# Five of eight gate products on GpSimd instead of three

## The reference

```python
# window attention: 8x8 windows, 4 heads of 16 channels, relative bias
x = x + conv(_ln_c(x))           # qkv, softmax(q k^T * scale + bias) v, w_proj, b_proj
# mixture of experts on the 64-channel tokens
t = _to_tokens(x)
router_probs = softmax(_ln_t(t) @ router_w + router_b)
top_p, top_i = top_k(router_probs, 2);  top_p = top_p / sum(top_p)
expert_out = einsum('bnd,edc->bnec', _ln_t(t), expert_w) + expert_b
t = t + einsum('bnk,bnkc->bnc', top_p, gathered expert_out)   # 8 experts, 2 per token
```

## Time and profile before

| | |
|---|---|
| three runs | 1201.91, 1205.79 (median), 1210.96 us |
| profiled execution, own time | 1205.98 us |
| its span | 1204.0 us |
| granted TensorE clock, mean | 0.977 |
| PE busy | 1052.5 us (87%) |
| DVE busy | 890.6 us (74%) |
| ACT busy | 745.5 us (62%) |
| POOL busy | 418.6 us (35%) |

### The profile page before, as it was taken

How to read it: one execution, slowest core, us unless ns; L and a number is a source line. 1 busy time by engine, 2 the same in 40 slices (tenths; PEclk the granted TensorE clock), 3 DMA queues, 4 the chain that set the end, 5 groups by cost and what they waited for, 6 DMA issues and landing times.

```text
span 1204.0 us, 39111 instructions
## 1 busy us (share of the span) xinstructions
PE 1052.5 (87%) x16838; PEld 605.8 (50%) x16838; DVE 890.6 (74%) x1443; ACT 745.5 (62%) x1217; POOL 418.6 (35%) x421
## 2 busy tenths in 40 slices
PE   1588889999999999999998999899998999899754
PEld 1355555555554555555554555555554555555311
DVE  3246687688878877788877867789877877788652
ACT  0257776677766766777766666767766766766400
POOL 0000244333443234333344234333443244333543
PEclk9999999999999999999999999999999999999778
DMA  5000656677878766677777757677878766677887
GB/s 179 2 1 20 150 131 149 157 179 183 194 179 196 170 163 155 170 174 179 188 186 186 174 138 170 158 176 188 196 177 194 163 159 167 165 159 173 182 195 172
DMA packets 49255, 192.48 MB, mean 160 GB/s; under 512 B 10558, under 2 KB 10814, under 8 KB 32572
## 3 DMA queue, kind: packets, MB, share of 16 engines
q1 hardware_dynamic: 49084, 189.98, 66.4%
HBM read 154.04 MB, written 18.87 MB: 144 GB/s over the span
## 4 chain that ended last, share of the span: by engine, by line
PE 83%; issue 8%; DMA 3%; DVE 3%; POOL 2%; ACT 1%; SPq 1%; POOLq 0%; DVEq 0%; ACTq 0%
PE bank L591 18%; PE bank L491 12%; PE bank L506 11%; PE bank L482 6%; PE bank L523 6%; PE bank L469 5%; PE bank L530 5%; PE bank L442 5%; PE bank L541 3%; DMA gz<-gates_dram 2%; PE bank L550 2%; PE bank L568 2%; PE bank L577 2%; PE bank L418 2%; PE bank L433 1%
## 5 line engine op out<-in xcount | busy, mean ns | idle before, releaser
L591 PE MATMUL bank<-gz,wex 64*64 64x512 f32 x2048 | 259.9, 612 | 11.1 <-DVE ob L1053 10.9
L900 POOL TENSOR_TENSOR gz<-gz,tt 128x1024 f32<-128x1024 f32 x96 | 233.6, 2435 | 79.3 <-DMA gz<-gates_dram 79.3
L1029 DVE TENSOR_TENSOR probs<-bank,mx 128x1024 f32<-128x1024 f32 x128 | 156.7, 1225 | 114.1 <-PE bank L506 111.2
L741 ACT ACTIVATE pt<-bank 128x512 f32<-128x512 f32 x256 | 151.8, 593 | 143.3 <-PE bank L506 143.0
L1044 DVE TENSOR_TENSOR gz<-gz,tt 128x1024 f32<-128x1024 f32 x160 | 198.9, 1261 | 13.1 <-DMA gz<-gates_dram 13.1
L872 POOL TENSOR_TENSOR tt<-prj,xs 128x512 f32<-128x512 f32 x64 | 80.6, 1283 | 355.8 <-ACT prj L758 355.8
L1022 DVE TENSOR_REDUCE mx<-bank 128x16 f32<-128x1024 f32 x128 | 156.2, 1220 | 40.6 <-PE bank L491 39.5
L506 PE MATMUL bank<-cst,probs 128*128 128x128 f32 x1024 | 167.3, 286 | 2.9 <-issue 2.0
L491 PE MATMUL bank<-km,qs 32*64 32x128 f32 x4096 | 149.9, 282 | 13.4 <-issue 13.4
L506 PEld LDWEIGHTS bank<-cst,probs 128*128 128x128 f32 x1024 | 113.0, 142 | 84.6 <-issue 74.4
L491 PEld LDWEIGHTS bank<-km,qs 32*64 32x64 f32 x4096 | 116.2, 136 | 62.8 <-issue 62.8
(11 more groups left out here) (111 smaller groups left out, 1423.9 us busy)
## 6 DMA issues: line engine op xcount, KB each, us to landing
gz<-gates_dram SPq DMA_DIRECT2D x256, 512.0 KB, 9.0
xs<-in_x SPq DMA_DIRECT2D x32, 512.0 KB, 8.9
tx<-tt SPq DMA_DIRECT2D x128, 128.0 KB, 2.8
out<-ob SPq DMA_DIRECT2D x128, 128.0 KB, 10.0
gz<-in_rel SPq DMA_DIRECT2D x1, 2048.0 KB, 9.9
gates_dram<-gt_rs SPq DMA_DIRECT2D x32, 64.0 KB
cst<-in_consts SPq DMA_DIRECT2D x1, 359.0 KB, 3.0
tt<-in_weights SPq DMA_DIRECT2D x4, 64.0 KB, 2.6
```

Source lines behind the costliest of these rows:

```text
L591: last = mm(bank[64 * x:64 * x + 64, Y_BANK + a, :], wex[64 * a:64 * a + 64, e, :], gz[64 * a:64 * a + 64, s.pair(e)[1], e % 2, x * CH:(x ...
L741: af(pt[g % 2][:, u % 2, :, :, :, :].rearrange("p j h x q -> p (j h x q)"), bank[:, PT_BANK, :], ACT.Copy).then_inc(pt_ready, 1)
L900: tt_(gz[:, k, e % 2, :], gz[:, k, e % 2, :], tt[s.buf(4)][:, :], op=ALU.mult).then_inc(z_pool, 1)
L1029: tt_(probs[g % 2][:, :, :, :].rearrange("p h w (m k) -> p (h w m) k", k=N), two_banks(S_BANK).rearrange("p (c k) -> p c k", k=N), mx[g % ...
```

## The change

Products 3 and 6 go from VectorE to GpSimd. On GpSimd, 6 is put ahead of 7 and 3 behind 1. On VectorE, product 5 and the last `normalise` of a strip are issued at the end of the step in which they become possible instead of at the start of the next one; product 3's place there is gone.

```diff
-        POOL_Z = [1, 4, 7]
+        POOL_Z = [1, 3, 4, 6, 7]
...
                 if s[6].on:
+                    gated(s[6], 6)
                     gated(s[6], 7)
                 if s[5].on:
                     gated(s[5], 1)
+                    gated(s[5], 3)
...
                 s = st.strips()
-                if s[4].on:
-                    normalise(s[4], 3)
-                if s[6].on:
-                    gated(s[6], 5)
                 if s[3].on:
                     row_max(s[3], 3)
...
-                if s[6].on:
-                    gated(s[6], 6)
                 if s[4].on:
                     move_logits(s[4])
...
                     gated(s[5], 2)
-                    gated(s[5], 3)
+                if s[3].on:
+                    normalise(s[3], 3)
+                if s[5].on:
+                    gated(s[5], 5)
```

## The result

Over several runs the changed kernel took 1255.55 us in the median (1249.11 to 1261.01), the kernel before 1203.85 us (1195.08 to 1210.96); the ratio is 1.0431, with an interval of 1.0338 to 1.0525. It is 52 us slower. The profiled execution took 1261.01 us against 1205.98, with a span of 1259.2 us: 55.2 us more. The forecast was 1263.

A forecast was written before the change was run, and what follows sets the result against it. TensorE was taken to bound the kernel, with 83% of the chain that ended last. 29 steps x 2.6 = 75 us, plus 2, less 20 coming back, gave 57 us on 1205.98: 1263 us, range 1235 to 1292.

The forecast's parts named there:

- Step 1: VectorE: two products leave, off TensorE's path, where VectorE waits for TensorE anyway; worth 0.
- Step 2: Product 6 on GpSimd ahead of 7: product 1 starts later, vr released later, keys late; +0.3 us a step (0 to 0.5).
- Step 3: Product 3 on GpSimd holds an instruction of VectorE's top-2 chain, delaying shift and group 1's scores; 2.3 us a step.
- Step 4: VectorE's product 5 and normalise 3 at the end of the step; 0.
- Step 5: GpSimd's sum: two products more, 4.7 us a step, against 10.35 us idle ahead of place_gates; 0.
- What comes back: TensorE's mid-group waits, taken as late instructions, hidden by the new wait: 20 of 22.7 us back (0 to 23).
- The sum: Whole kernel: 2.6 us in 29 steps, 75 us, plus 2, less 20 given back: 57 us slower, 1263 us.
- rival C: Collision as forecast, and TensorE's clock falls: 25 us more if every second step pays, 1288; every step 1312; 12%.
- Rival A: VectorE keeps the port while instructions are queued, GpSimd's products wait, waits ahead of L482 vanish: 1176, faster; 4%.
- Rival B: Product 3 misses the top-2 chain and runs beside row_max and shift, which are not held: 1206 to 1215; 7%.

The follow-up runs named there:

- experiment 4: Kernel before, three products on GpSimd, with GpSimd's product 1 moved behind place_gates: 1169.99 us, ratio 0.9773.
- experiment 6: Changed kernel with GpSimd's products 1 and 3 both moved behind place_gates: 1174.47 us, ratio 0.9778 to the kernel before.
- experiment 3: Kernel before with VectorE's new order alone, all five products staying on VectorE: 1201.20 us, ratio 1.0026.
- experiment 2: Kernel before with product 3 alone moved to GpSimd, behind product 1: 1238.85 us, ratio 1.0361.
- experiment 5: Changed kernel with GpSimd's product 3 moved behind place_gates: 1211.67 us, ratio 1.0086 to the kernel before.
- experiment 7: Changed kernel with product 3 replaced by two equally long GpSimd memsets that read nothing from SBUF: 1216.37 us, ratio 1.0126 to the kernel before.

## Why the prediction was right

**Step 1 (VectorE's two products are worth 0)** held. The wait for TensorE ahead of shift 3 grew from 3.09 to 3.62 us, and experiments 4 and 6 give the same time with three and with five products on GpSimd.

**Step 2 (product 6, +0.3 us a step).** Size about right, the way there another: L1000 does not slip in between 6 and 7 but loses the seam and is held for a whole product. So mq does not pass at the next seam, with vr held in its place, as the step had it; mq is asked for later and is itself held for 1.92 us. In the step shown, TensorE's wait for the keys is 1.21 us; over 23 waits it is 1.2 us (28.3), not the 1.5 that I expected. The keys are later by 0.22 us (scores of group 0 start 12.62 us behind the residual in the median of 26 steps, 12.40 before), but so is part of TensorE's work ahead of them. By itself the step cost 13 us where 29 x 0.3 gave 9.

**Step 3 (product 3, +2.3 us a step)** held in mechanism and was a little too large. From the start of group 0's scores to that of group 1's a step took 6.91 us in the median of 26 steps, 4.88 before: 2.03, not 2.3. The chain itself, from its first instruction (L1096 here) to the end of its eleventh, took 5.59 us in the mean of the 29 steps, 3.53 before: 2.06, with an instruction held in 28 of them. The 2.3 had allowed too little for what passes at the start of a product: a reduce there is not held, and the instruction behind it, 0.29 us alone, took 2.0 to 2.5 us. Experiments 2, 5 and 7 show the mechanism: the product there, elsewhere, and there without its reads.

**Step 4 (the new order, 0)** is experiment 3, ratio 1.0026. **Step 5 (GpSimd's sum, 0)** held: 6.09 us are left ahead of place_gates.

**What comes back.** I took 20 of the 22.7 us of mid-group waits; they shrank to 0.5 us, by 22. With the new wait they are gone in experiment 2 as well (1.4 us), without it they are there (21.1 us in experiment 4, 20.1 in experiment 7). That they are late instructions is borne out by the instruction queue, which I had not laid beside them. It moves packets of 16 KB, some 9 us apart. The DMA view of 217.3 to 218.6 us in the kernel before has one (packets, MB, share of 16 engines' time):

```profile
q8 instruction: 1, 0.02, 5.5%
```

It ends at 218.46, inside the wait that ends at 219.88. Up to 1160 us the kernel before has 17 mid-group waits of over 0.3 us. All of them end 1.3 to 1.7 us behind the end of such a packet, and the three that are left in the changed kernel 1.45 to 1.47 us behind one.

**The sum.** The 29 steps run from the start of the residual in step c = 5 to that in c = 34. TensorE's busy time in them (stretch, us, busy of PE, PEld, DVE, ACT and POOL, granted clock, DMA share, GB/s), before and after:

```profile
134.00:1111.10 977.10, 909.83 (x14928) 529.39 (x14928) 786.37 (x1269) 669.71 (x1097) 367.25 (x376) 0.99 0.73 173
131.50:1164.40 1032.90, 936.00 (x14928) 546.88 (x14928) 831.53 (x1212) 672.43 (x1097) 503.86 (x434) 0.97 0.69 163
```

The same 14928 matmuls took 55.8 us more: TensorE was idle for 29.6 us more (67.3 before, 96.9 after) and busy for 26.2 us more. The idle part first, by the waits in these stretches, before and after:

```profile
PE bank L482 <- issue: 32.0, 26, 2.3
PE bank L491 <- issue: 13.4, 7, 2.7
PE bank L523 <- issue: 10.2, 6, 2.8
```
```profile
PE bank L482 <- DVE probs L1031: 53.7, 28, 3.4
PE bank L482 <- issue: 35.0, 26, 3.1
PE bank L491 <- issue: 3.3, 2, 1.8
PE bank L523 <- issue: 0.5, 1, 0.5
```

The wait for the shift brought 53 us where the sum had 29 x 2.3 = 67, the keys 3 where it had 9, and 26 us of waits within TensorE's own stream came back where it had 20 (30.9 us before, 4.6 after, with the small groups that are not shown). So the forecast's terms were worth 30 us and not 55.

The other 26 us are the term that I put at nothing and gave to rival C: the clock. The mean granted clock fell from 0.977 to 0.958, and was 0.958 to 0.964 in all four runs. At the level of 1.2 GHz the core spent 2 x (1 - 0.958) x 1259 = 106 us instead of 2 x (1 - 0.977) x 1204 = 55. Nearly all of that lies in the 29 steps: the clock records there have 58.0 us at this level against 10.2, while the granted clock behind them is alike (0.80 against 0.79 before). Half of the 47.8 us of difference, 24 us, is what work at half the rate costs more, if TensorE is busy throughout, and it nearly covers the 26 us. The 47.8 us are as much as 14 stretches of 3.4 us, one in every second step.

One such stretch begins just behind the new wait of the step above:

```profile
646.00:650.00 4.00, 3.65 (x69) 2.79 (x70) 3.42 (x10) 1.16 (x2) 1.51 (x4) 0.70 0.96 232
```

The L491 matmuls behind that wait took 1.47 us where a group otherwise takes 1.10:

```profile
647.01 1.47 PE L491 MATMUL bank<-km,qs 32*64 32x128 f32 x32
```

Of the ten that begin between 200 and 1100 us in the changed kernel, two begin inside a wait for the shift, of 3.2 and 3.4 us, and eight 0.9 to 1.7 us behind the end of one. How many such stretches the waits bring is not fixed, and the trace of experiment 2 shows what the waits cost nearly without them:

```profile
132.00:1136.80 1004.80, 913.36 (x14928) 531.18 (x14928) 812.43 (x1240) 672.56 (x1097) 437.98 (x405) 0.99 0.71 168
```

It has the new wait too, and the clock records have only 20.5 us at 1.2 GHz in these 29 steps. They took 27.7 us more than in the kernel before, 24.2 idle and 3.5 busy. The other three executions of experiment 2 ran at a lower mean clock, 0.964 to 0.970 against 0.974, and took 6 to 14 us longer. No experiment set the clock by itself, so its part is read from traces and not tested.

So the hold on the chain was right and its size nearly so, but what I held against rival C was wrong: its clock came at its lower price, every second step, 25 us, in the execution that was traced. The time of rival C, 1288, did not come, because the waits were worth 25 us less than my sum. That 1263 came out near the mark, 1261.01 in the profiled execution, is in good part luck: two errors of 25 us and more pull in opposite directions. Rivals A and B did not occur: in 28 of the 29 steps an instruction of the chain was held behind a product.

## What to carry to other kernels

## What the runs showed of the hardware that I had not expected

- At a seam between two GpSimd products it counts who came first. In the step shown, the guard is asked for at 631.59, just as product 6 makes room for 7, and loses; it is held for 2.46 us, and at the next seam, where it has been waiting, it ends 0.15 us behind product 7 and ahead of product 1's end. At the earlier trace rows, asked for earlier, it took only 0.62 us. The place at a seam decides between 0.3 and 2.5 us.
- The mid-group waits of TensorE, some 22 us in 900, vanish when TensorE stands still for 2 us shortly before, so about a third of the cost of product 3 was paid for by them. Each ended 1.3 to 1.7 us behind a packet of the instruction queue.
- A new wait of 2 us in a step can cost more than its own length: in the changed kernel each of the ten stretches at 1.2 GHz that began between 200 and 1100 us began in such a wait or within 1.7 us behind it. The 29 steps had 48 us more at this level than before, some 24 us of cost by the estimate above; in experiment 2, with the same wait, only 10 us more.
- The mean granted clock of an execution does not tell what the clock cost; where the slow stretches lie does. Product 6 alone took 1209.49 us at a mean clock of 0.955 and 1209.45 us at 0.978; in the first of these the clock was 0.77 in the first 133.5 us and 0.99 in the 29 steps. Runs of the kernel before ranged from 0.952 to 0.983 on the chips of the experiments. Only one execution of the changed kernel was traced, so how much its clock took from the other three stays open.
